# Another order of turns, weighted values and scores in the attention units of a two-layer kernel

## The reference, cut to what matters

```python
xn = _layernorm(x)
x = x + _L0_attn_ref(xn, ...) + _L0_ffn_ref(xn, ...)   # 8 heads, windows of 128; 8 experts, best 2
xn = _layernorm(x)
x = x + _L1_attn_ref(xn, ...) + _L1_ffn_ref(xn, ...)   # gated attention; 32 experts, best 8
```

```python
sim = jnp.einsum('bwie,bwje->bwij', bq, bk)            # scores, own window and its neighbours
sim = jnp.where(mask, NEG, sim)
attn = jax.nn.softmax(sim, axis=-1)
out = jnp.einsum('bwij,bwje->bwie', attn, bv)          # weighted values
```

## Time and profile before

| | us |
|---|---|
| median of 3 runs (lowest, highest) | 1027.35 (1027.15, 1031.48) |
| the profiled execution | 1027.42 |
| its span, first to last instruction | 1026.1 |
| PE busy (4440 products) | 990.7, 97% |
| DVE busy | 656.5, 64% |
| ACT busy | 506.6, 49% |
| POOL busy | 428.5, 42% |
| mean granted clock of PE | 0.998 of full |

### The profile page before, as it was taken

How to read it: one execution, slowest core, us unless ns; L and a number is a source line. 1 busy time by engine, 2 the same in 40 slices (tenths; PEclk the granted TensorE clock), 3 DMA queues, 4 the chain that set the end, 5 groups by cost and what they waited for, 6 DMA issues and landing times.

```text
span 1026.1 us, 13382 instructions
## 1 busy us (share of the span) xinstructions
PE 990.7 (97%) x4440; PEld 619.8 (60%) x4440; DVE 656.5 (64%) x1553; ACT 506.6 (49%) x1193; POOL 428.5 (42%) x339
## 2 busy tenths in 40 slices
PE   5999999999999999999999999999999999999998
PEld 2655555675656756566555666556665566656655
DVE  4956758586664876658766577656776466724933
ACT  3654663625645266452664536545464544645222
POOL 4865337550084402753036520465206541044333
PEclk9999999999999999999999999999999999999999
DMA  7150310610423004220232302232023220243061
GB/s 269 33 144 1 115 42 1 136 42 11 125 65 92 22 25 114 72 82 21 70 89 73 82 1 94 66 92 63 7 88 86 65 60 11 85 105 82 22 154 33
DMA packets 34564, 72.78 MB, mean 71 GB/s; under 512 B 4544, under 2 KB 5312, under 8 KB 34112
## 3 DMA queue, kind: packets, MB, share of 16 engines
q1 hardware_dynamic: 33072, 69.03, 24.5%
q10 hardware_dynamic: 1424, 2.90, 0.8%
HBM read 69.04 MB, written 2.88 MB: 70 GB/s over the span
## 4 chain that ended last, share of the span: by engine, by line
PE 90%; DVE 5%; issue 2%; ACT 2%; DMA 0%; POOL 0%; DVEq 0%; ACTq 0%; POOLq 0%
PE ps L598 12%; PE ps L701 12%; PE ps L461 9%; PE ps L463 9%; PE ps L462 9%; PE ps L510 6%; PE ps L523 5%; PE ps L535 5%; PE ps L676 3%; PE ps L606 3%; PE ps L485 3%; PE ps L492 2%; PE ps L647 2%; PE ps L456 1%; PE ps L655 1%
## 5 line engine op out<-in xcount | busy, mean ns | idle before, releaser
L1102 ACT ACTIVATE wide<-ps 128x512 f32<-128x512 f32 x136 | 81.1, 596 | 220.2 <-PE ps L463 219.7
L1031 ACT ACTIVATE pw<-ps,w_cols 128x512 f32<-128x512 f32 x144 | 98.6, 687 | 110.0 <-PE ps L463 108.5
L1798 POOL TENSOR_TENSOR atc<-atc,wide 128x512 f32<-128x512 f32 x64 | 82.0, 1283 | 148.2 <-DVE atc L1544 148.2
L991 ACT ACTIVATE pw<-ps,nmax 128x256 f32<-128x256 f32 x256 | 118.1, 471 | 47.5 <-DVE nmax L1338 47.4
L598 PE MATMUL ps<-pw,w_w 128*128 128x512 f32 x288 | 136.1, 595 | 0.0
L1780 POOL TENSOR_TENSOR kr<-qks,w_rope 128x512 f32<-128x512 f32 x32 | 43.5, 1361 | 193.4 <-DVE qks L1316 193.4
L1349 DVE COPY pt<-ps 128x512 f32<-128x512 f32 x128 | 85.5, 681 | 29.6 <-PE ps L523 28.6
L1338 DVE TENSOR_REDUCE nmax<-ps 128x4 f32<-128x1024 f32 (+1 forms) x80 | 79.2, 1007 | 31.9 <-PE ps L510 31.9
L1415 DVE SCALAR_TENSOR_TENSOR pt<-ps,w_cols,wb 128x512 f32<-128x512 f32 x64 | 47.7, 746 | 77.6 <-PE ps L598 52.2
L461 PE MATMUL ps<-yc,eg 128*128 128x512 f32 x128 | 96.6, 755 | 0.0
L523 PE MATMUL ps<-ident,pw 128*128 128x128 f32 x512 | 82.3, 283 | 13.3 <-DVE pt L1349 8.4
(11 more groups left out here) (204 smaller groups left out, 2063.7 us busy)
## 6 DMA issues: line engine op xcount, KB each, us to landing
wb<-scratch SPq DMA_DIRECT2D x128, 256.0 KB, 4.0
wb<-scratch SPq DMA_DIRECT2D x32, 512.0 KB, 5.3
wide<-scratch SPq DMA_DIRECT2D x16, 512.0 KB, 5.9
xin<-in_x SPq DMA_DIRECT2D x8, 256.0 KB, 2.8
out<-wide SPq DMA_DIRECT2D x8, 256.0 KB, 2.1
w_w<-in_w ACTq DMA_DIRECT2D x1, 1152.0 KB, 11.3
wb<-in_w SPq DMA_DIRECT2D x1, 1152.0 KB, 11.9
w_ed<-in_ed SPq DMA_DIRECT2D x1, 1024.0 KB, 16.9
```

Source lines behind the costliest of these rows:

```text
L991: m = act.activation(pw[:, u % 2, j, :], ps[:, score_bank(u, par), qt * SEQ:(qt + 1) * SEQ], ACT.Exp, bias=nmax[:, u % 3, j:j + 1], scale= ...
L1031: act.activation(hid[:, n % 4, :], bank(UPS0[n % 2]), ACT.Gelu, bias=cols[:, C_B1 + 2 * e + c:C_B1 + 2 * e + c + 1], scale=1.0).then_inc(* ...
L1798: pool.tensor_tensor(hh[h], hh[h], sgl[:, (c + 1) % 3, :], ALU.mult).then_inc(*HH_POOL.one)
```

## The change

On PE, for u from 1 on, `weigh(s, u - 1)` moves from between the two turns of unit u to ahead of both; the scores of unit u + 2 follow the second turn as before. That holds for all of step 1 and, in steps 2 to 7, from u = 3 on. Step 0 keeps its order. At the start of steps 2 to 7: `scores(s, 2)` leaves `experts1` and stands between the two turns of unit 0; `rows1` comes after the second turn of unit 0 instead of between the two; `weigh(s, 0)` comes after the scores of unit 3; `weigh(s, 1)` stays between the turns of unit 2. DVE and ACT follow: `maxima(s, 2)` sits between the two copies of unit 0, `out_rows` after it and the second copy, and `out_cols(s, 0)` after both exponentials of unit 2. No instruction is added or removed.

```diff
 # PE, attention(s)
                 for u in range(UNITS):
+                    if u and (second or s > 1 and u > 2):
+                        weigh(s, u - 1)
                     turn(s, u, 0)
+                    if u and first or u == 2 and s > 1:
+                        weigh(s, u - 1)
+                    if u == 0 and s > 1:
+                        scores(s, 2)
+                    turn(s, u, 1)
                     if u == 0 and s > 1:
                         rows1(s - 2, 1)
-                    if u:
-                        weigh(s, u - 1)
-                    turn(s, u, 1)
                     if 0 < u < UNITS - 2 or u == 0 and s < 2:
                         scores(s, u + 2)
+                    if u == 1 and s > 1:
+                        weigh(s, 0)
 # PE, end of experts1(s)
-                if more:
-                    scores(n, 2)
-                else:
+                if not more:
                     rows1(x, 1)
 # ACT, attention(s)
-                    if u > 1:
+                    if u > 2 or u == 2 and s < 2:
                         out_cols(s, u - 2)
...
                     exps(s, u, 1)
+                    if u == 2 and s > 1:
+                        out_cols(s, 0)
 # DVE, attention(s)
-                if s > 1:
-                    out_rows(s - 2, 1)
                 for u in range(UNITS):
                     pt_copy(s, u, 0)
+                    if u == 0 and s > 1:
+                        maxima(s, 2)
                     pt_copy(s, u, 1)
                     if 0 < u < UNITS - 2 or u == 0 and s < 2:
                         maxima(s, u + 2)
+                    if u == 0 and s > 1:
+                        out_rows(s - 2, 1)
                     invert(s, u)
 # DVE, end of experts1(s)
                     maxima(n, 1)
-                    maxima(n, 2)
```

## The result

| | before | after |
|---|---|---|
| median of 5 runs each, us (lowest, highest) | 1027.36 (1027.15, 1031.48) | 1022.09 (1020.45, 1022.56) |
| ratio (95% interval) | | 0.994 (0.9923 to 0.9956) |
| profiled execution and its span | 1027.42, 1026.1 | 1020.45, 1019.1 |
| a step, 3 to 4 | 124.65 | 123.66 |
| step 1, scores of unit 1 to turned denominators | 35.85 | 36.69 |

The kernel is 5.3 us faster by the medians.

What follows compares the result with a forecast made beforehand. PE, busy 97% of the span and carrying 90% of the chain, was taken as the bound. Six steps at 1.02 (6.1 us) plus 0.6 in step 1 made 6.7 us: 1020.7 us from 1027.35, range 1018.0 to 1025.3.

Steps and rivals of the forecast that it cites:

- Start of the steps: Start of steps 2 to 7: PE's 1.22 wait for DVE's copies becomes 0.77; a gain of 0.75 a step.
- Shape changes: Changes of the stationary operand's shape on PE: three per unit instead of four, 0.15 less per regular unit.
- regular units: Attention units without a wait for another engine: 3.32 instead of 3.47; units 3 and 5 gain 0.15 each.
- Scores to weigh, the unknown: Scores directly followed by a weigh, some 26 times: no extra cost taken, bounds -2.6 and +5.2 us.
- Unit 4: Unit 4 of steps 2 to 7: second turn still waits for exponentials on ACT; 3.99 instead of 4.05, gain 0.06.
- Units 6 and 7: Units with halves of `up0` in place of scores: cover too short by 0.4 at the second weigh, loss 0.09.
- Step 1: Unit 4 of step 1: the weigh falls into PE's 0.92 wait for exponentials; scores 0.6 earlier, kept afterwards.
- The slower rival: Copies late at every weigh behind the scores: 0.37 wait at 43 weighs, 15.9 us, 1036.6 us; chance 8%.
- The cover of 0.23: Regular units: PE reaches the weigh 2.30 after the first turn starts, copies allow it at 2.07; 0.23 to spare.
- The clock: Half-clock stretch of 3.30 us after step 1's gelu wait may vanish or another come: about 1.7 us either way.

## Why the prediction was right, and where not

The forecast was 1020.7, the measured median 1022.09, inside the range. The 1.4 us between them are as much as step 1 went wrong (0.6 gained expected, 0.84 lost). In steps 2 to 7 the account held. I expected 1.02 a step, it is 0.99; 6 times that is 5.9 of the forecast 6.1.

- *Start of the steps*: 0.75 expected, 0.69 in the trace (12.68 from the scores of unit 1 to the end of those of unit 4, 13.37 before), 0.68 with this part alone. The wait came out as laid on the clock (second turn of unit 1 1.22 after the first, of which 0.78 wait, 0.77 expected). The missing 0.06 is at the weigh of unit 1, which starts 0.65 after the turn, not 0.59 (370.01 to 370.66). For the start of the steps I had asked only when `out_rows` empties bank 1. But ACT's copy of the weigh of unit 0 empties it too, and runs from 370.13 to 370.51; PE goes on 0.15 later, as it goes on 0.14 after the same copy in step 1 (115.09 to 115.23).
- *Shape changes*: regular units 3.32, as computed. Scores to weigh, the unknown, costs nothing extra (1.38).
- *Unit 4* gains 0.01, not 0.06. The second pair of exponentials holds its turn just as long, and so the scores stand 2.67 after `turn_weights0` in both traces (375.48 + 1.38 = 376.86, next scores at 379.53).
- *Units 6 and 7* lose nothing, where I had 0.09 lost to a short cover. The wait at the weigh is there (0.24; I had 0.4, in part because I let PE resume 0.10 after the copies, and it resumes 0.05 after them: 387.23 to 387.28), but it lies beside a longer chain on ACT, which ends 5.70 after the scores of unit 7 in any order; my sum followed PE alone.
- *Step 1* is the step of the prediction that failed, in two places. It said that "in the new order the weigh falls into the wait", and a gain of 0.6 "which the rest of the step keeps"; 0.84 was lost. First, a weigh needs bank 1 empty as well as its copies. I had noted that condition for the start of the steps, but did not follow ACT's order for it here. With bank 1 emptied early the forecast gain is there behind unit 4 (0.61). Second, the step does not keep it. In unit 7 a projection of layer 1 waits for the copy of a turn that the new order has moved next to it, 0.61 in all; with the old order in unit 7 and bank 1 emptied early, 0.56 stays. The weighs of units 2 and 3 also wait for both copies (0.92 and 0.34), where the old order had a turn in front that needed one. By the scores behind unit 4 that costs nothing more: they stand at 19.97 with these waits and at 20.02 without them.
- *The slower rival* (copies late at every weigh) shows in units 2 and 3 of step 1 and, as foreseen, at the weigh of unit 6. The cover of 0.23 held in every regular unit of steps 2 to 7.
- *The clock*: the drop came and went by 1.6 us, as bounded, on both kernels.

The sum in the trace: 5.9 gained in steps 2 to 7, 0.84 lost in step 1, 1.6 from the clock and 0.25 because the scores of unit 1 in step 1 stand that much earlier (96.38 for 96.63), in all 6.9 of the 7.0 between the spans. The 0.25 is chance: the change leaves the part before them alone, and in the other traces with one drop or none these scores stand at 96.00 to 97.02. The medians hold none of the clock's share and stand 5.3 apart.

## What to carry to other kernels

When an operation is moved into another's wait, list every condition that it has itself, its output buffer too, and place each on the engine that fulfils it. An engine that is 97% busy may still lose time between instructions: compare start-to-start distances of the same work with different neighbours, and group work of one operand shape. Before a gain or loss at one wait is booked, ask whether another chain ends at the same point; removing a wait of 0.24 here moved nothing.

## What the runs showed of the hardware

- In these f32 products, one whose stationary operand has another shape than the one before has its load start 0.17 to 0.39 us after the loads before it, together with the product itself (370.91 and 370.92 in the earlier trace rows). Between products of one shape the load starts 0.11 ahead of its product (366.98 and 367.09), while the products before run. That made one turn 0.44 or 0.59 by its neighbours. A turn ahead of a half of `up0`, whose operand has the turn's shape but whose product is four times as wide, keeps to 0.40, which speaks for the shape of the operand; no run changed that shape alone.
- The clock of PE fell to its lower level of 1.2 GHz (0.50 over a stretch of 3.30 us) right after an idle of 2.36 us in step 1, in some executions of the same kernel and not in others. Of the eleven traces with that idle six have the drop and take 105.70 to 105.75 us from the turned denominators of step 1 to the scores of unit 1 in step 2; five have none and take 104.09 to 104.15. So one drop costs 1.6 us. The idle alone does not explain it: one trace has a second drop in step 0, after waits of 0.25 to 0.51 us, and the other traces have waits of these sizes there too, without a drop. No drop followed the waits of 1.2 to 1.3 us.
